# Attention plus experts on one core: the loop over attention chunks written out on four engines

## The chip, the core and the metric

The kernel runs on one core of a Trainium2 chip. The metric is the device time of one execution in microseconds, as the median of several executions. A core has five engines that run their own instruction streams side by side: TensorE (PE in the profile, with PEld for the loads of its stationary operand), VectorE (DVE), ScalarE (ACT), GpSimd (POOL) and SyncE (SP, which here issues DMAs). Each has a sequencer that reads instructions ahead of the engine it feeds; the profile marks rows of a sequencer with a q (PEldq, DVEq). Engines wait for one another through semaphores alone.

## What is computed

One transformer layer over 2048 tokens of width 512. First an attention with a decaying state, then a mixture of 12 experts of which each token takes two. Cut to what matters:

```python
xn = layernorm(x, gamma, beta)
w = sigmoid(xn @ Wx @ Ww + bw); k = xn @ Wk; v = xn @ Wv; r = sigmoid(xn @ Wr)
# 8 heads of 64; one step for each token
def step(state, inp):
    state = (1.0 - wt)[..., None] * state + kt[..., None] * vt[..., None, :]
    y = einsum('bhs,bhst->bht', rt, state)
    return (state, y)
x = layernorm(x + ys @ Wo)
x = layernorm(x + sum over the token's two experts e of cw[e] * (silu(x @ w1[e].T) * (x @ w3[e].T)) @ w2[e].T)
```

## The kernel before

The recurrence is computed in 16 chunks of 128 tokens (`NT` = 16). Two chunks make a pair (`NPAIR` = 8), and the projections of x to decay, key, receptance and value are made for a pair at a time, two or more chunks ahead of their use. On TensorE a call of `chunk` does, for chunk n: the scores of its tokens against each other, by levels of distance (`scores`, L299, 32 products for half of the heads, twice), the reading of the state (L309), the turning of the keys (L329), the output projection of chunk n-1 (L349), the product of scores and values (`apply_values`, L319) and the update of the state (L337). Between these it places the projection jobs of a later pair (`job`, L259 and L270 to L278). Odd chunks take the list `FIRST` (the transposes, then decay and key), even ones the list `SECOND` (receptance and value).

The other engines run their own loop over the same chunks: ScalarE copies out of PSUM and applies sigmoids (`kbT<-pM` at L685 stands once in each chunk), VectorE masks the scores (L831), forms the products of decays (L538, once for a pair) and the levels of receptance (L547, L555), GpSimd forms the levels of the key (L571). ScalarE and GpSimd also split pieces of the expert weights into two halves of 16 bits, three pieces for each chunk; SyncE loads and stores these pieces in a loop of its own (L234).

The order on each engine is the order of the program, and what binds the engines are waits on semaphores with growing counts: the n-th chunk waits for a count that is a multiple of n. Chunk 0 stands ahead of the loop, chunks 13, 14 and 15 behind it. Chunks 1 to 12 are a loop of three rounds with four chunks in its body on TensorE (L427), ScalarE (L779) and VectorE (L936); GpSimd, which works a chunk ahead, has the loop for its chunks 2 to 13 (L964). These are loops of the machine: the body stands once in the program, an engine's register holds the round, each wait on a count and each address that depends on the round is worked out in registers, and at the end of the body a compare-and-branch goes back to its start, twice, and falls through the third time. The experts (from L1137) have loops of the same kind, L1276 on TensorE with 10 rounds, L1492 on VectorE and L1326 on ScalarE with 20, L1568 on GpSimd with 8.

Of the kernel before, what the change touches and what calls it, by code (L numbers as in the profile page):

```python
# [26 lines left out]
NPAIR = T // PAIR  # L27
# [41 lines left out]
def attention(nc, X, idt, kc, gw, x, wxT, ww, wk, wv, wr, wo, by_feature, ident, masks, consts, gate_w, w_experts, w_split, logitT):  # L69
# [9 lines left out]
    with ExitStack() as ctx:  # L79
# [167 lines left out]
        def _(pe):  # L247
# [121 lines left out]
            def chunk(n, k, jobs=None):  # L369

                q, par, slots = jobs or (None, None, [[]] * 5)

                def fill(s):
                    for m in slots[s]:
                        job(q, m, par)
                    if isinstance(n, int) and n in GATE_SLOTS:
                        for u in GATE_SLOTS[n][s]:
                            gate_step(u)
                pe.wait_ge(r_dec, n * NL + (NL - 1))
                pe.wait_ge(r_kept, n * (NL - 2) + (NL - 2))  # L380
                pe.wait_ge(k_dec, n * NL + (NL - 1))
                pe.wait_ge(k_kept, n * (NL - 1) + (NL - 1))
                scores(n, k, 0)
                read_state(n, k)
                turn_keys(n, k)
                if slots is FIRST:
                    job(q, 0, par)
                    job(q, 1, par)
                else:
                    fill(0)  # L390
                if not isinstance(n, int) or n:
                    attend_out(n - 1)
                else:
                    pe.wait_ge(kb_out, 1)
                    pe.sem_inc(m_full, 1)
                if slots is FIRST:
                    fill(0)
                apply_values(n, k, 0)
                scores(n, k, 1)
                fill(1)  # L400
                write_state(n, k)
                fill(2)
                fill(3)
                apply_values(n, k, 1)
                fill(4)
# [18 lines left out]
            pe.wait_ge(setup_done, 1)  # L424
            pe.wait_ge(w_in[5], 16)
            chunk(0, 0, (1, 1, SECOND))
            with pe.Fori(0, (NPAIR - 2) // 2) as j:  # L427
                for u in range(2):
                    chunk(j * 4 + (2 * u + 1), 2 * u + 1, (j * 2 + (2 + u), u, FIRST))
                    chunk(j * 4 + (2 * u + 2), 2 * u + 2, (j * 2 + (2 + u), u, SECOND))  # L430
# [86 lines left out]
        def act_piece(a, n, k, t):  # L517

            _, buf, loaded = piece_of(n, k, t)
            a.wait_ge(piece_in[buf], loaded)  # L520
            if not isinstance(loaded, int) or loaded > 16:
                a.wait_ge(piece_out[buf], loaded - 16)
            a.copy(piece_parts[buf][:, 0, :], piece[buf][:, :]).then_inc(piece_hi, 1)  # L523
# [56 lines left out]
        def pool_chunk(g, n, k, q):  # L580

            for lv in range(NL):
                pool_level(g, n, k, q, lv)
                if lv in PIECE_AT:
                    pool_piece(g, n, k, PIECE_AT.index(lv))
# [3 lines left out]
        def _(a):  # L589
# [186 lines left out]
                        act_piece(a, 0, 0, PIECE_AT.index(at - 5))  # L776
            a.wait_ge(stat1, 9)
            chunk(0, 0, 0, 0, (1, 1, SECOND))
            with a.Fori(0, (NPAIR - 2) // 2) as j:  # L779
                for u in range(2):  # L780
                    q, pair = j * 2 + (2 + u), j * 2 + (1 + u)
                    chunk(j * 4 + (2 * u + 1), 2 * u + 1, j * 2 + u, pair, (q, u, FIRST))
                    chunk(j * 4 + (2 * u + 2), 2 * u + 2, pair, pair, (q, u, SECOND))
# [6 lines left out]
        def _(v):  # L790
# [142 lines left out]
                if lv == 0:  # L933
                    low_x(1, 1)
            chunk(0, 0, nxt=0)
            with v.Fori(0, (NPAIR - 2) // 2) as j:  # L936
                for u in range(2):
                    q, pair = j * 2 + (2 + u), j * 2 + (1 + u)
                    chunk(j * 4 + (2 * u + 1), 2 * u + 1, pair, (q, u))
                    chunk(j * 4 + (2 * u + 2), 2 * u + 2, pair)  # L940
# [12 lines left out]
        @block.gpsimd  # L953
        def _(g):
            for i, name in ((1, "r"), (2, "v")):
                g.wait_ge(w_hi, i + 1)
                g.tensor_tensor(wl[name][:, :, :], staged[name][:, :, :], wh[name][:, :, :], ALU.subtract).then_inc(w_lo[name], 1)

            for name in "krv":
                g.wait_ge(w_lo[name], 1)  # L960
            g.wait_ge(wz_full, KT)
            for n in range(2):
                pool_chunk(g, n, n, 0)
            with g.Fori(0, (NPAIR - 2) // 2) as j:  # L964
                for k in range(2, 6):
                    pool_chunk(g, j * 4 + k, k, j * 2 + k // 2)
            for n in range(NT - 2, NT):
                pool_chunk(g, n, n, n // 2)
# [691 lines left out]
```

## Time and profile before

| what | value |
|---|---|
| runs | 856.07, 857.55 and 864.34 us, median 857.55 |
| the profiled execution | 859.21 us, of which the span of instructions is 857.4 |
| TensorE busy | 725.9 us, 85% of the span |
| VectorE, ScalarE, GpSimd busy | 498.7, 342.1 and 328.7 us |
| granted TensorE clock, mean over the span | 0.932 |
| chunks 1 to 12 (starts of L685, n1 to n13) | 94.45 to 418.54 us |
| expert rounds | about 548 to 796 us |

The profiled execution is 1.7 us above the median of the runs. Times in the rows are microseconds from the start of the span, and durations of single instructions are in nanoseconds where a row says min/median/max. A granted clock of 1.00 is TensorE at its full 2.4 GHz and 0.50 is 1.2 GHz.

### The profile page before, as it was taken

Reading aid. Unit: us, or ns where it says so; the run is one execution under the profiler, and the core shown is the slowest. Engines: PE = TensorE matmul, PEld = TensorE weight load, DVE = VectorE, ACT = ScalarE, POOL = GpSimd, SP = SyncE. Lnnn points to the kernel's source line nnn. Section 1 sums busy time; section 2 is a strip of 40 time slices with the busy share of each in tenths; the row PEclk is TensorE's granted clock in tenths of the full one; section 3 lists DMA queues with packets and bytes.
Section 4 is the critical chain, followed back from the end, with each engine's and each line's share of the span. In section 5 each row is a group of like instructions: output and inputs, shape, how many; then the busy total and the mean of one; then the engine's idle time right before and its main releaser. Section 6 shows DMA issues by size and latency. Waiting matters only on the chain. (4 is left out here: it accounts for less than half of the span.)

```text
span 857.4 us, 18313 instructions
## 1 busy us (share of the span) xinstructions
PE 725.9 (85%) x6030; PEld 525.2 (61%) x6031; DVE 498.7 (58%) x1035; ACT 342.1 (40%) x675; POOL 328.7 (38%) x355
## 2 busy tenths in 40 slices
PE   5879999998999989999969861799999999999400
PEld 2658787876877769778636521466666666666200
DVE  4655867666677646775756558244445444444285
ACT  4454645546345444554466220222222222222154
POOL 0345534542445425454244002243343434333262
PEclk9999999998999989999969975799999999999855
DMA  8615345431454324433342066144466557322394
GB/s 339 225 37 165 117 127 149 148 106 45 149 148 133 105 62 149 141 106 99 101 148 78 22 224 266 50 158 143 165 217 234 197 183 245 122 95 89 134 336 155
DMA packets 38867, 126.75 MB, mean 148 GB/s; under 512 B 3984, under 2 KB 4368, under 8 KB 36496
## 3 DMA queue, kind: packets, MB, share of 16 engines
q1 hardware_dynamic: 31920, 103.31, 35.7%
q0 software_dynamic: 6880, 22.55, 7.7%
q8 instruction: 42, 0.69, 0.3%
q14 instruction: 25, 0.20, 0.1%
HBM read 81.02 MB, written 44.83 MB: 147 GB/s over the span
## 5 line engine op out<-in xcount | busy, mean ns | idle before, releaser
L831 DVE COPY_PREDICATED ST<-msk,pS 128x256 f32<-128x256 uint8 x224 | 121.1, 569 | 100.1 <-issue 65.9
L577 POOL TENSOR_TENSOR piece_parts<-piece,piece_parts 128x1024 f16<-128x1024 f32 x48 | 104.6, 2179 | 115.5 <-ACT piece_parts L523 115.5
L571 POOL TENSOR_TENSOR L<-L,AM 128x256 f32<-128x256 f32 x96 | 70.9, 738 | 118.4 <-ACT L L515 108.8
L1236 PE MATMUL pH<-ring,xgh 128*128 x344 | 104.5, 304 | 5.3 <-issue 2.8
L1237 PE MATMUL pH<-ring,xgh 128*128 x344 | 104.1, 303 | 0.0
L1238 PE MATMUL pH<-ring,xgl 128*128 x344 | 104.1, 303 | 0.0
L299 PE MATMUL pS<-L 64*128 64x64 f32 x1536 | 99.2, 276 | 1.8 <-issue 1.7
L1552 POOL DMA_INDIRECT y_scratch<-ysb,sidx x43 | 42.9, 998 | 136.3 <-DVE ysb L1478 136.3
L299 PEld LDWEIGHTS pS<-L 64*128 64x128 f32 x1536 | 93.6, 192 | 2.1 <-issue 2.1
L1462 DVE TENSOR_TENSOR hid<-pH,sil 128x320 f32<-128x320 f32 x43 | 21.1, 492 | 119.6 <-ACT sil L1315 119.6
L555 DVE TENSOR_TENSOR L<-L,AM 128x256 f32<-128x256 f32 x96 | 70.6, 735 | 16.1 <-ACT L L502 10.0
L1315 ACT ACTIVATE sil<-pH 128x320 f32<-128x320 f32 x43 | 18.8, 437 | 131.0 <-PE pH L1238 131.0
L349 PE MATMUL pM<-w_o,yT 128*128 128x512 f32 x128 | 59.8, 611 | 4.3 <-ACT yT L724 2.8
L523 ACT CAST piece_parts<-piece 128x1024 f16<-128x1024 f32 x48 | 50.1, 1043 | 24.4 <-DMA piece<-in_w_experts 24.4
L1539 POOL DMA_INDIRECT xg<-x_scratch,gidx x43 | 42.7, 994 | 34.0 <-POOL gidx L1536 30.8
L1254 PE MATMUL pO<-ring,hTh 128*128 x129 | 49.0, 380 | 1.8 <-DVE hTh L1473 1.4
L1255 PE MATMUL pO<-ring,hTh 128*128 x129 | 48.9, 379 | 0.0
L1236 PEld LDWEIGHTS pH<-ring,xgh 128*128 128x128 f16 x344 | 34.0, 99 | 24.3 <-issue 11.1
L502 ACT COPY L<-L 128x256 f32<-128x256 f32 x80 | 32.5, 407 | 38.2 <-DVE L L555 26.9
L1311 ACT CAST hTh<-pHT 128x384 f16<-128x384 f32 x43 | 20.6, 479 | 63.9 <-PE pHT L1244 63.9
L1478 DVE COPY ysb<-pO 128x512 f32<-128x512 f32 x43 | 29.7, 692 | 23.0 <-PE pO L1255 23.0
L1237 PEld LDWEIGHTS pH<-ring,xgh 128*128 128x128 f16 x344 | 33.9, 99 | 13.4
(206 smaller groups left out, 1623.6 us busy)
## 6 DMA issues: line engine op xcount, KB each, us to landing
piece<-in_w_experts SPq DMA_DIRECT2D x48, 512.0 KB, 5.5
w_split_scratch<-piece_parts SPq DMA_DIRECT2D x48, 512.0 KB, 3.9
ring<-w_split_scratch SPq DMA_DIRECT2D x12, 2048.0 KB, 8.6
yin<-y_scratch SPq DMA_DIRECT2D x16, 512.0 KB, 5.8
x_scratch<-X SPq DMA_DIRECT2D x1, 4096.0 KB, 14.1
out_x<-X SPq DMA_DIRECT2D x8, 512.0 KB, 2.8
X<-in_x SPq DMA_DIRECT2D x1, 3072.0 KB, 23.3
X<-in_x SPq DMA_DIRECT2D x2, 512.0 KB, 7.5
```

The lines of the kernel that those rows point to most:

```text
L299: i = pe.matmul(o, k_, r_, start=True, stop=True)
L349: i = pe.matmul(pM[:, 0, :], yT[:, g, :], w_o[:, g, :], start=(g == 0), stop=(g == KT - 1))
L523: a.copy(piece_parts[buf][:, 0, :], piece[buf][:, :]).then_inc(piece_hi, 1)
L555: v.tensor_tensor(next_grown(k, lv, 1), grown(rec, k, lv, 1), factor(c, lv, 0), ALU.mult).then_inc(r_dec, 1)
L571: g.tensor_tensor(next_kept(k, lv, 0), kept(key, k, lv, 0), by, ALU.mult).then_inc(k_dec, 1)
L577: g.tensor_tensor(piece_parts[buf][:, 1, :], piece[buf][:, :], piece_parts[buf][:, 0, :], ALU.subtract).then_inc(piece_lo, 1)
L831: v.copy_predicated(out[:, :, :, 0 if lv == 0 else 1, :], msk[:, lv, :, :].rearrange(shape, m=m), pS[:, :, lv * S:(lv + 1) * S].rearrange( ...
L1236: pe.matmul(p[:, 0, 0:F], xgh[par][:, k, :], wh, start=(k == 0), stop=False)
L1237: pe.matmul(p[:, 0, 0:F], xgh[par][:, k, :], wl, start=False, stop=False)
L1238: t = pe.matmul(p[:, 0, 0:F], xgl[par][:, k, :], wh, start=False, stop=(k == KT - 1))
L1254: pe.matmul(pO[:, 0, :], hTh[:, k, :], wh, start=(k == 0), stop=False)
L1255: t = pe.matmul(pO[:, 0, :], hTh[:, k, :], wl, start=False, stop=(k == FT - 1))
```

## The change

In the four engines' programs the loop of the machine is replaced by a loop of Python, so that each of the twelve chunks stands in the program with its own numbers. SyncE's program and the expert loops stay as they are.

```diff
@@ TensorE
-            with pe.Fori(0, (NPAIR - 2) // 2) as j:
+            for j in range((NPAIR - 2) // 2):
                 for u in range(2):
                     chunk(j * 4 + (2 * u + 1), 2 * u + 1, (j * 2 + (2 + u), u, FIRST))
                     chunk(j * 4 + (2 * u + 2), 2 * u + 2, (j * 2 + (2 + u), u, SECOND))
@@ ScalarE
-            with a.Fori(0, (NPAIR - 2) // 2) as j:
+            for j in range((NPAIR - 2) // 2):
@@ VectorE
-            with v.Fori(0, (NPAIR - 2) // 2) as j:
+            for j in range((NPAIR - 2) // 2):
@@ GpSimd
-            with g.Fori(0, (NPAIR - 2) // 2) as j:
+            for j in range((NPAIR - 2) // 2):
                 for k in range(2, 6):
                     pool_chunk(g, j * 4 + k, k, j * 2 + k // 2)
```

The start of a round on TensorE before the change. These rows stand once in the program and are reached from chunk 0 and, twice, from the branch at the end of the body:

```order
L427 UNCONDITIONAL_BRANCH
L427 ISA
L380 ISA [waits r_dec]
L382 ISA [waits k_dec,r_kept]
L285 ISA [waits k_kept]
L299 MATMUL pS<-rec,key 128x64 [waits s_dve]
L299 MATMUL pS<-rec,key 128x64
L299 MATMUL pS<-rec,L 128x64 x2
L299 MATMUL pS<-L 128x64 x12
```

And the end of the body, behind the last projection job of the round:

```order
L316 REGISTER_ALU
L319 MATMUL pY<-ST,val 64x128 [waits s_dve]
L319 MATMUL pY<-ST,val 64x128 x3
L427 REGISTER_ALU
L427 COMPARE_AND_BRANCH
```

The same place after the change, between chunks 4 and 5. `ISA` rows at the head of a chunk are sequencer instructions that wait or set registers; the branch and they are gone, and the waits sit on the first matmul of the scores:

```order
L278 MATMUL pA<-wh_v,xl 128x512
L319 MATMUL pY<-ST,val 64x128 [waits s_dve]
L319 MATMUL pY<-ST,val 64x128 x3
L299 MATMUL pS<-rec,key 128x64 [waits k_kept,k_dec,s_dve,r_kept,r_dec]
L299 MATMUL pS<-rec,key 128x64
L299 MATMUL pS<-rec,L 128x64 x2
```

No matmul has moved against another. On VectorE the end of the body stood like this:

```order
L872 TENSOR_TENSOR state<-pM,sdec 64x4x64
L880 ISA [waits x1_ready]
L880 BN_STATS stats<-X 128x6
L936 REGISTER_ALU
L936 COMPARE_AND_BRANCH
```

and the branch led to the products of decays, with a register instruction ahead of nearly each of them:

```order
L936 ISA
L531 ISA [waits a_out]
L538 TENSOR_TENSOR AM<-dec 128x512 [waits r_dec,k_dec]
L535 ISA
L538 TENSOR_TENSOR AM<-AM 128x256 [waits am_ready]
L535 REGISTER_ALU
L538 TENSOR_TENSOR AM<-AM 128x128 [waits am_ready]
```

After the change these two pieces join, and what is left between them are the operations themselves:

```order
L872 TENSOR_TENSOR state<-pM,sdec 64x4x64
L880 BN_STATS stats<-X 128x6 [waits x1_ready]
L538 TENSOR_TENSOR AM<-dec 128x512 [waits r_dec,k_dec,a_out]
L538 TENSOR_TENSOR AM<-AM 128x256 [waits am_ready]
L538 TENSOR_TENSOR AM<-AM 128x128 [waits am_ready]
```

Here too the order of the operations is the same as before; only the branch, the register arithmetic and the separate waits have gone. SyncE's rows are the same in both programs.

## Rows read from the trace of the kernel before

**Rows 1.** The page: span, granted TensorE clock in 40 slices, TensorE's instruction queue.

```profile
span 857.4 us, 18313 instructions
...
PEclk9999999998999989999969975799999999999855
...
q8 instruction: 42, 0.69, 0.3%
```

**Rows 2.** Timeline of ScalarE, 60 to 300: start, us, what, idle before, releaser.

```profile
204.05 0.59 ACT L685 COPY kbT<-pM 128x512 f32<-128x512 f32 x1 [5.39 <-PE pM L329]
```

**Rows 3.** Windows between starts of L685: length, busy by engine, PEclk, DMA share, GB/s.

```profile
121.47:146.46 24.99, 24.99 (x246) 18.78 (x245) 18.44 (x35) 12.77 (x26) 11.65 (x10) 1.00 0.44 127
146.46:173.48 27.02, 26.21 (x278) 21.91 (x277) 17.82 (x29) 14.32 (x31) 12.25 (x10) 1.00 0.37 118
173.48:204.05 30.57, 27.46 (x246) 21.00 (x245) 18.87 (x37) 12.94 (x26) 11.21 (x10) 0.90 0.36 106
...
231.13:256.12 24.99, 24.99 (x246) 18.77 (x245) 18.71 (x35) 12.77 (x26) 11.67 (x10) 1.00 0.45 128
256.12:283.15 27.03, 26.22 (x278) 21.93 (x277) 17.85 (x29) 14.33 (x32) 12.28 (x10) 1.00 0.37 118
283.15:314.51 31.36, 28.36 (x246) 21.88 (x245) 18.59 (x37) 12.93 (x26) 11.27 (x10) 0.89 0.36 104
...
393.55:418.54 24.99, 24.95 (x244) 18.51 (x242) 19.18 (x35) 11.44 (x25) 11.70 (x10) 1.00 0.43 128
418.54:452.04 33.50, 24.65 (x202) 16.82 (x203) 18.70 (x43) 19.72 (x37) 11.54 (x10) 0.80 0.30 95
```

**Rows 4.** Line L427 on TensorE's sequencer: duration min/median/max in ns, first to last start.

```profile
L427 PEldq COMPARE_BRANCH  x3: 76/3638/5121, 190.4 to 410.5; - x3
```

**Rows 5.** Line L936 on VectorE's sequencer, 297 to 307.

```profile
L936 DVEq COMPARE_BRANCH  x1: 63/63/63, 299.0 to 299.0; - x1
L936 DVEq FUSED_REGOPS  x1: 85/85/85, 304.9 to 304.9; - x1
```

**Rows 6.** Line L779 on ScalarE's sequencer, 297 to 307.

```profile
L779 ACTq FUSED_REGOPS  x1: 78/78/78, 303.2 to 303.2; - x1
```

**Rows 7.** Timeline of TensorE, 188 to 204.

```profile
194.62 0.44 PE L299 MATMUL pS<-rec,key 64*128 64x64 f32 x4 [1.42 <-issue]
...
199.18 1.98 PE L299 MATMUL pS<-L 64*128 64x64 f32 x17 [1.68 <-issue]
201.09 2.07 PE L309 MATMUL pY<-L,state 128*128 128x128 f32 x8
```

**Rows 8.** Timeline of TensorE, 142 to 149.

```profile
144.83 1.16 PE L309 MATMUL pY<-L,state 128*128 128x128 f32 x8
```

**Rows 9.** Timeline of VectorE, 138 to 204.

```profile
138.33 1.40 DVE L538 TENSOR_TENSOR AM<-dec 128x512 f32<-128x512 f32 x1
...
194.38 0.69 DVE L538 TENSOR_TENSOR AM<-dec 128x512 f32<-128x512 f32 x1 [3.96 <-issue]
```

**Rows 10.** Windows behind the two taken back branches (columns of Rows 3).

```profile
198.10:204.90 6.80, 5.72 (x35) 5.60 (x35) 2.99 (x6) 1.41 (x4) 0.66 (x1) 0.50 0.01 2
307.30:314.10 6.80, 6.71 (x53) 6.43 (x50) 3.26 (x9) 0.74 (x2) 0.66 (x1) 0.50 0.03 11
```

**Rows 11.** DMA queues that load instructions, 560 to 790: packets, MB, share.

```profile
q8 instruction: 1, 0.02, 0.0%
q14 instruction: 2, 0.02, 0.0%
```

**Rows 12.** Lines of the expert loops' branches on TensorE's and VectorE's sequencers.

```profile
L1276 PEldq COMPARE_BRANCH  x10: 76/207/238, 571.6 to 788.0; - x10
...
L1492 DVEq COMPARE_BRANCH  x20: 50/56/74, 567.5 to 795.6; - x20
```

**Rows 13.** Waits of TensorE, 80 to 470: total us, times, longest.

```profile
PE pA L270 <- DVE xl L816: 4.5, 6, 0.8
```

**Rows 14.** Line L316 on TensorE's sequencer.

```profile
L316 PEldq ALU_OP  x24: 32/32/32, 100.3 to 408.6; - x24
```

## The prediction

> **What bounds the kernel now.** I began with the page [rows 1]: the span is 857.4 us, and and the granted clock is at full speed from the first slice to the 20th, with two exceptions, a digit 8 in the tenth and one in the fifteenth. Each slice is 21.4 us, so these lie near 200 and 310 us, in the midst of the attention chunks. Such a dip is a place to look. Next I cut the stage at an event that occurs once in each chunk, ScalarE's copy at L685, of which there are 16 from 71.79 to 474.51 (one is shown in [rows 2]), and asked for the busy time between them [rows 3]. The reader should compare lengths of like chunks. A stretch from the copy of an even chunk to that of the next odd one lasts 24.99 us, and TensorE is busy for all 24.99 of it; a stretch that starts in an odd chunk lasts 27.02 with 26.21 busy. So inside a round TensorE is the bound, at full clock. Two stretches are out of line, and they are the two that hold a taken back branch: 30.57 us (chunk 4 to 5) and 31.36 us (chunk 8 to 9). The third even stretch at the end of a round, 12 to 13, has the branch that falls through, and lasts 24.99 like the rest.
>
> **Why those two are long.** TensorE's branch instruction itself [rows 4]: of its three executions one took 76 ns, the others 3638 and 5121 ns. On VectorE the branch record is short, but the next sequencer instruction came at 304.9 behind a branch at 299.0, 5.9 us later [rows 5]; ScalarE, whose branch came at 303.0, went on at 303.2 [rows 6]. Then the timelines. TensorE stood idle for 1.42 us ahead of the first scores of the new round and for 1.68 us in the midst of them [rows 7], neither put down to another engine. Behind that gap its matmuls ran slowly: the same eight state reads took 2.07 us [rows 7] against 1.16 in an ordinary chunk [rows 8]. The granted clock in the 6.8 us behind each gap was 0.50, the 1.2 GHz level [rows 10], after TensorE had stood idle at the branch. VectorE sat idle 3.96 us ahead of its first product of decays, where in the round before it went on without a gap [rows 9].
>
> **What is removed.** The price of a taken back branch needs no model, since the same chunk without one is in the same trace. First: 30.57 - 24.99 = 5.58 us. Second: 31.36 - 24.99 = 6.37 us. The busy column says what they are made of. Idle time: 30.57 - 27.46 = 3.11 and 31.36 - 28.36 = 3.00. Work made longer by the lower clock: 27.46 - 24.99 = 2.47 and 28.36 - 24.99 = 3.37. The sums agree with the 5.58 and 6.37 [rows 3]. All of it is on the path, because TensorE is the engine that is never idle in the ordinary stretch, so **11.95 us** go. VectorE's stall goes with it and takes nothing more: it waits for TensorE's scores there in any case. The loop's entry and its fall-through cost 0: the stretch 12 to 13 is no longer than its like [rows 3].
>
> The queue of TensorE's instructions moved 42 packets in all [rows 1], and only one in the 230 us of the expert rounds [rows 11], whose ten branches took at most 238 ns [rows 12]: a short loop is not loaded again, and the long one is. The Trainium skill, page "Runtime: NRT & Kernel Launch", section "Instruction fetch mechanics", says that a taken branch to code which the sequencer no longer holds must wait until that code is fetched by DMA; by that rule the change takes away just these waits, and the trace agrees with it.
>
> **What is added.** Nothing that executes. But the code of chunks 5 to 12 is now new code, loaded once each, instead of the body passed again. The bound comes from the first round, which even before the change was code passed for the first time: its stretches of 24.99 and 27.02 us equal those of the second round, 24.99 and 27.03 [rows 3]. So a straight passage through fresh instructions hides its loads; I take 0, and at the far end 0.01 us for each of the eight chunks, 0.1 us.
>
> **What else goes: register arithmetic and separate waits.** TensorE's 24 additions at L316 took 32 ns each [rows 14], 0.8 us if every one were on the path, and the other engines shed some such instructions ahead of most operations. In the even stretches TensorE has no idle time at all, so nothing can be gained there. In the odd ones it waits for the low part of x, 0.8 us at most, 4.5 us over six chunks [rows 13], on a chain through ScalarE and VectorE. I take 0, because this chain's operations run back to back; the far ends are a gain of 4.5 us and the loss of 0.1 that stands above. The fourth and longest stretch, 33.50 us with a mean clock of 0.80 [rows 3], is chunk 13, which stood outside the loop already. It keeps its code, but starts 12 us earlier, and where its low-clock time falls may change. By the two stretches above, one such lapse made work 2.47 to 3.37 us longer; I take 0 and keep 3.4 us to either side.
>
> **The sum.** 857.4 - 11.95 = 845.4 us of span, and 859.2 - 11.95 = 847.3 us for the profiled execution. That one stood 1.7 us above the median; for the median I forecast 857.55 - 11.95 = **845.6 us**, a gain of 1.4%. What comes after the attention is a chain in which nothing waits for a fixed time, so it should begin 12 us sooner and last as long.
>
> **Rivals.**
> *The full gain and more.* ScalarE and VectorE, with their register instructions gone, close TensorE's wait in the odd chunks too: 845.6 - 4.5 = 841.1. Against it: the wait is one of operations and not of issue. Chance 0.07.
> *A lapse of the clock in its place.* A gap in chunk 13, or behind it, costs one more stretch at the lower clock: 845.6 + 3.4 = 849.0. For it: the digits 6, 7, 5 and 7 between the 21st and the 26th slice [rows 1] say that this region has several. Chance 0.10.
> *The gap is no matter of the branch.* The expert pieces' transfers run at the same time, and TensorE's gap might stay with them. Then 857. Against it, the stretches without a branch have such transfers as well (GB/s of 118 to 128 against 104 and 106) and no gap [rows 3]. Chance 0.04. To the same time leads a rule of price: if a taken branch cost what a fall-through does, 76 ns, the change would give 0.2 us, 857.4. The Trainium skill, page "Advanced Engine Details and Errata", section "Control Flow Timing", gives about 108 ns for a compare-and-branch; the 3638 and 5121 ns here are far off that, and the 207 ns of the expert loop are near it. So I give the rule nothing for these two branches.
> *Slower: the expert loops are reloaded.* The written-out program is longer, so the expert loops stand at other places in the instruction stream. They are short enough now to stay loaded [rows 11, 12]; if one of them came to lie so that its start is lost at each round, each of TensorE's nine taken branches at L1276 would cost 5.58 to 6.37 us, 50 to 57 us: 896 to 903. Break-even is at two such branches. Against it: each body keeps its length, and over ten and twenty passes the queues brought one packet for TensorE and two for all others together, so there seems to be room to spare. Chance 0.03. Straight code that starves where the loop did not, with more than 12 us lost, gets 0.02: the first round speaks against it.
> The forecast, 845.6 within some 2 us, has the remaining 0.74.
>
> **How the numbers follow.** No change cannot be told from a change of less than 1% in this kernel, 8.6 us. The forecast and the first rival lie beyond that. The lapse rival, at 849.0, is 8.55 us faster and splits evenly: 0.05 to either side. Faster than 848.97 therefore has 0.74 + 0.07 + 0.05 = 0.86, of which I take off 0.02 for the scatter of the runs (856.07 and 857.55 are 1.5 us apart), 0.84. Within 1% has 0.05 + 0.04 + 0.02 = 0.11, and slower 0.05. The range must reach the forecast and the two nearby rivals: down to 841.1, up to 849.0, and 0.5 us of scatter at the upper end, 841 to 849.5.
>
> **What would show it.** In the changed kernel's profile the even stretches between L685 copies, 4 to 5 and 8 to 9, should be 25.0 us with TensorE busy throughout and a clock of 1.00; the idle times of 1.42, 1.68 (TensorE) and 3.96 us (VectorE) should be gone; TensorE's instruction queue should still show some 40 packets. Copies n5 and n9 should start at 198.5 and 302.6 us, n13 at 406.6. The forecast is wrong if a stretch of straight code is longer than its like, if the odd stretches shrink, if chunk 13 takes other than 33.5 us, or if the expert rounds on VectorE no longer last the (795.6 - 567.5) / 19 = 12.0 us of [rows 12].

## The result

The changed kernel runs in 846.68 us (median of 4 runs, 845.40 to 846.88), the kernel before in 856.97 us (median of 4, 856.07 to 864.34). The ratio of the runs is 0.9846 with a 95% interval of 0.9805 to 0.9887, faster by 1.5%; the two medians alone are 10.29 us or 1.2% apart. Forecast were 1.4% and 845.6 us. Compared again with more runs (`e11_after_again`), the two stood at 847.65 and 858.61 us, 10.96 us apart, ratio 0.9868, interval 0.9837 to 0.9899. One execution of the kernel before, timed beside `e12_pe_both`, took 1274.15 us at a mean granted clock of 0.577 and enters no number below. The profiled execution took 846.87 us with a span of 844.6; 847.3 and 845.4 were forecast for it.

The page of the changed kernel, the lines that answer to [rows 1]:

```profile
span 844.6 us, 17397 instructions
...
PEclk9999999999999999999979975899999999999755
...
q8 instruction: 37, 0.61, 0.3%
```

The 8 in the tenth slice and the one in the fifteenth are gone. TensorE's instruction queue (q8) moved 37 packets where it had moved 42: the code is longer, and less of it is loaded. `e4_two_rounds` below shows that this count goes with the taken branches.

ScalarE's copies L685 cut the stage as before. The windows between them, with the columns of [rows 3]:

```profile
174.04:199.03 24.99, 24.99 (x246) 18.79 (x245) 18.38 (x35) 12.76 (x27) 11.65 (x10) 1.00 0.41 128
199.03:226.05 27.02, 26.22 (x278) 21.91 (x277) 17.86 (x29) 14.31 (x32) 12.16 (x10) 1.00 0.35 118
...
278.06:303.05 24.99, 24.99 (x246) 18.77 (x245) 18.14 (x35) 12.75 (x27) 11.66 (x10) 1.00 0.41 128
...
407.07:441.53 34.46, 25.07 (x202) 16.25 (x203) 18.55 (x43) 19.71 (x37) 11.53 (x10) 0.80 0.28 92
```

The two stretches of 30.57 and 31.36 us now last 24.99 each, TensorE busy in all of it. Odd stretches kept their 27.02. From copy n1 to copy n13 the stage took 418.54 - 94.45 = 324.09 us before and 407.07 - 95.00 = 312.07 now, 12.02 less.

TensorE's timeline where the first back branch was, to be read beside [rows 7] and [rows 8]; the idle time would stand in brackets at the end of a row, and there is none:

```profile
193.09 0.66 PE L319 MATMUL pY<-ST,val 128*64 128x128 f32 x8
193.68 0.44 PE L299 MATMUL pS<-rec,key 64*128 64x64 f32 x4
...
197.40 1.16 PE L309 MATMUL pY<-L,state 128*128 128x128 f32 x8
```

And VectorE's, which had stood idle for 3.96 us here [rows 9]:

```profile
190.26 0.69 DVE L880 BATCH_NORM_STATS2 stats<-X 128x6 f32<-128x512 f32 x1
190.87 1.30 DVE L538 TENSOR_TENSOR AM<-dec 128x512 f32<-128x512 f32 x1
```

The expert loops were not disturbed by their new place, as the branch row of TensorE shows beside [rows 12]:

```profile
L1276 PEldq COMPARE_BRANCH  x10: 76/208/226, 559.4 to 774.8; - x10
```

### The profile page after: what moved, and what is told of

Read it like the earlier page. It is cut to its first block and busy times, and to the rows that moved or that the text cites. A ratio compares the mean times of both kernels' runs of the same rounds, so it can differ in the third digit from the quotient of the medians.

```text
span 844.6 us, 17397 instructions
## 1 busy us (share of the span) xinstructions
PE 718.4 (85%) x6030; PEld 519.4 (61%) x6031; DVE 497.3 (59%) x1035; ACT 341.4 (40%) x675; POOL 328.1 (39%) x355
## 5 line engine op out<-in xcount | busy, mean ns | idle before, releaser
L299 PE MATMUL pS<-L 64*128 64x64 f32 x1536 | 96.2, 271 | 0.0
L299 PEld LDWEIGHTS pS<-L 64*128 64x128 f32 x1536 | 91.1, 188 | 0.0
L1236 PEld LDWEIGHTS pH<-ring,xgh 128*128 128x128 f16 x344 | 33.8, 98 | 24.8 <-issue 11.5
L270 PE MATMUL pA<-xh,wh_z 128*128 128x256 f16 x128 | 34.9, 273 | 8.6 <-DVE xl L816 4.8
```

Of the source, the lines that this page charges most:

```text
L299: i = pe.matmul(o, k_, r_, start=True, stop=True)
L1236: pe.matmul(p[:, 0, 0:F], xgh[par][:, k, :], wh, start=(k == 0), stop=False)
```

## The experiments

All were timed beside the kernel before. Since a few microseconds are at stake, each is also read by the time from copy n1 to copy n13, in which the loop lies; it is 324.09 us before the change and 312.07 after it, and the later stages don't enter it. It is known for one execution of each kernel, the profiled one. `e7_light_loads` and `e10_light_straight` leave most of the expert weights out of the computation.

| kernel | median us | ratio (interval) | n1 to n13 | stretch 4 to 5 | stretch 8 to 9 |
|---|---|---|---|---|---|
| before | 857.0 to 859.1 | 1 | 324.09 | 30.57 | 31.36 |
| change | 846.68 | 0.9846 (0.9805 to 0.9887) | 312.07 | 24.99 | 24.99 |
| e11_after_again | 847.65 | 0.9868 (0.9837 to 0.9899) | 312.08 | 24.99 | 24.99 |
| e1_pe_only | 847.03 | 0.985 (0.9804 to 0.9896) | 313.01 | 25.28 | 24.99 |
| e2_dve_only | 858.40 | 0.9996 (0.997 to 1.0021) | 325.39 | 32.92 | 30.39 |
| e3_pe_dve | 846.85 | 0.9851 (0.9808 to 0.9894) | 312.07 | 24.99 | 24.99 |
| e4_two_rounds | 855.35 | 0.9942 (0.9913 to 0.9971) | 317.78 | 30.68 | 24.99 |
| e5_gap_long | 859.93 | 0.9997 (0.9964 to 1.003) | 328.46 | 33.14 | 33.21 |
| e6_gap_short | 849.89 | 0.988 (0.9834 to 0.9927) | 318.75 | 26.24 | 30.36 |
| e7_light_loads | 848.34 | 0.989 (0.9832 to 0.9948) | 315.56 | 26.65 | 26.82 |
| e10_light_straight | 842.87 | 0.981 (0.977 to 0.985) | 312.07 | 24.99 | 25.00 |
| e8_experts_out | 842.98 | 0.9805 (0.9768 to 0.9842) | 312.09 | 24.99 | 24.99 |
| e9_pe_experts | 843.66 | 0.9817 (0.9783 to 0.985) | 312.09 | 25.00 | 24.99 |
| e12_pe_both | 843.16 | 0.9819 (0.978 to 0.9859) | 312.62 | 25.00 | 24.99 |

### Which engine's branch

`e1_pe_only`: TensorE's loop alone is written out.

```diff
--- before
@@ TensorE
-            with pe.Fori(0, (NPAIR - 2) // 2) as j:
+            for j in range((NPAIR - 2) // 2):
```

> Only TensorE's loop is written out; VectorE, ScalarE and GpSimd keep theirs. Theory A (TensorE's own reload is the price): TensorE's idle times of 3.1 and 3.0 us and the low clock behind them go, the stretches between copies n4 to n5 and n8 to n9 fall from 30.57 and 31.36 to 25 us, and the time falls by 11 to 12 us, as with all four written out. Rival B (VectorE's reload is the price and TensorE's only lies beside it): VectorE still stalls 4 to 5 us ahead of its decay products, its masks come late, TensorE waits for them, and the gain is under 6 us. In ordinary stretches VectorE waits 2.4 us for the scores behind those products; a stall of 3.96 and 5.14 us is longer than that, so something between, a gain of 8 to 11 us with stretches of 25.5 to 27.5 us, would say that VectorE's stall was hidden by TensorE's and comes to light without it.

It had nearly the whole gain: 847.03 us. The first back branch's stretch and the one after it, and the same at the second:

```profile
173.68:198.96 25.28, 25.28 (x249) 19.08 (x248) 17.05 (x35) 12.89 (x26) 10.67 (x9) 1.00 0.40 127
198.96:226.37 27.41, 26.04 (x276) 21.62 (x274) 18.16 (x31) 14.50 (x32) 13.68 (x11) 1.00 0.36 116
...
303.37:330.66 27.29, 26.22 (x278) 21.92 (x277) 18.02 (x30) 14.51 (x32) 13.55 (x11) 1.00 0.37 117
```

The first branch's two stretches are 0.29 and 0.39 us above 24.99 and 27.02, and behind the second branch only one is longer, by 0.27 us: 0.95 us in all. VectorE in the same kernel shows where that comes from:

```profile
194.76 0.69 DVE L538 TENSOR_TENSOR AM<-dec 128x512 f32<-128x512 f32 x1 [4.15 <-issue]
...
198.29 1.32 DVE L831 COPY_PREDICATED ST<-msk,pS 128x256 f32<-128x256 uint8 x2
```

It still stalls at its own branch, for 4.15 us, and its masks begin without a wait of their own. So VectorE's pause was covered by TensorE's, and uncovered it is worth 0.68 and 0.27 us, where my band of stretches allowed 0.5 to 2.5 a branch.

`e2_dve_only`: the same edit on VectorE's loop alone.

> Only VectorE's loop is written out. Theory A: TensorE still reloads its code at both branches, nothing is gained, 0 to 1 us, and the two stretches stay at 30 to 31.4 us. Rival B: the stretches shrink by 3 us or more.

Nothing was gained, 858.40 beside 858.69 us. Of the two stretches one was longer than in the profile of before and one shorter:

```profile
174.29:207.21 32.92, 29.68 (x246) 23.36 (x245) 20.07 (x37) 12.85 (x26) 11.64 (x10) 0.84 0.33 99
...
286.24:316.63 30.39, 27.62 (x246) 21.11 (x245) 19.57 (x37) 12.85 (x27) 11.65 (x10) 0.89 0.38 106
```

The range of 30 to 31.4 that I wrote was too narrow for one of them. Four stretches with a taken branch, from two kernels, now read 30.4 to 32.9: the price of one such branch is 5.4 to 7.9 us and changes from pass to pass. The idle part is steadier, 32.92 - 29.68 = 3.24 and 30.39 - 27.62 = 2.77 us, beside 3.11 and 3.00 before; most of the difference is work at the lower clock. In the longer stretch the granted clock stood at 0.50 for 10.2 us (196.8 to 207.0), in the shorter one for 6.8 us (309.4 to 316.2).

`e3_pe_dve`: both edits, ScalarE's and GpSimd's loops kept.

> TensorE's and VectorE's loops are written out, ScalarE and GpSimd keep theirs. Theory A (with or without a hidden stall of VectorE): the full gain, 11 to 12.5 us, because the other two went through their branches within 0.3 us. A rival, that the gain came from register arithmetic on ScalarE and GpSimd, would leave a part of it out.

846.85 us and 312.07 us between the copies, the same as the change to the hundredth. The loops of ScalarE and GpSimd cost nothing.

`e4_two_rounds`: all four engines loop over two rounds, and the third is written out.

```diff
--- before
@@ TensorE, and in the same way ScalarE, VectorE and GpSimd
-            with pe.Fori(0, (NPAIR - 2) // 2) as j:
+            with pe.Fori(0, 2) as j:
                 ...
+            for j in range(2, 3):
+                for u in range(2):
+                    chunk(j * 4 + (2 * u + 1), 2 * u + 1, (j * 2 + (2 + u), u, FIRST))
+                    chunk(j * 4 + (2 * u + 2), 2 * u + 2, (j * 2 + (2 + u), u, SECOND))
```

> On all four engines the loop keeps two rounds, and the third is written out behind it: one taken back branch in place of two. If each taken branch has its price, about half of the gain: 5.6 to 6.4 us less than the kernel before, the stretch n4 to n5 at 30 to 31.5 us and n8 to n9 at 25.0. If the gain came from having constants in place of registers, the third round alone would have it, 4 us, and n8 to n9 would stay long.

One taken branch is left, and one long stretch:

```profile
L427 PEldq COMPARE_BRANCH  x2: 79/1768/3458, 190.3 to 300.0; - x2
```

```profile
173.35:204.03 30.68, 27.47 (x246) 21.00 (x245) 18.99 (x37) 12.95 (x27) 11.17 (x10) 0.90 0.38 106
...
283.08:308.07 24.99, 24.99 (x246) 18.78 (x245) 18.57 (x35) 12.76 (x26) 11.65 (x10) 1.00 0.44 128
```

TensorE's queue of instructions, on this kernel's page, stands between the 42 packets with two taken branches and the 37 with none:

```profile
q8 instruction: 39, 0.64, 0.3%
```

It is 42 as well in `e2_dve_only`, which keeps both of TensorE's branches, and 37 in `e1_pe_only` and `e3_pe_dve`, which have none. So a taken branch of TensorE back over the long body does load code again. The second queue of instructions, q14, moved 25 packets before the change and in `e1_pe_only`, and 17 in `e2_dve_only`, where VectorE's loop is gone: VectorE's branch does the same.

Between the copies it gained 324.09 - 317.78 = 6.31 us, as expected. The median gained only 858.69 - 855.35 = 3.3, less than I wrote; in the profiled execution chunks 13 and 14 took 58.85 us (412.10 to 470.95) where they took 55.97 before (418.54 to 474.51), which hides 2.9 us of the gain. That constants in place of registers made the gain is excluded: chunks 1 to 4 run on registers and chunks 9 to 12 on constants here, in the same 24.99 and 27.02 us.

### Is it the code or the pause

`e5_gap_long` and `e6_gap_short` take the written-out kernel and put a pause of TensorE alone where the branches were.

```diff
--- after
@@ TensorE, chunk
+                if n in (5, 9):
+                    pe.wait_ge(k_dec, (n + 1) * NL + 2)      # e5_gap_long
+                    pe.wait_ge(r_dec, (n + 1) * NL + 1)      # e6_gap_short
                 scores(n, k, 0)
```

(one of the two added waits in each kernel)

> The written-out kernel with a pause put in where the back branches were: ahead of the scores of chunks 5 and 9 TensorE also waits for GpSimd's second product for the next chunk, which in an ordinary round ends some 2.8 us later. No code is loaded again. If idle time alone drops the clock, as I read the kernel before, each pause costs its 2.8 us and 2.5 to 3.4 us of slower work: 10.6 to 12.4 us in all, back to 857 to 859. If the lower clock belonged to the reload, the two pauses cost 5.6 us and no more, about 852.

> The same with a shorter pause: ahead of the scores of chunks 5 and 9 TensorE waits for VectorE's first product of the next chunk, which ends about 1 us later. Expected: 2 us in all, with a clock of 1.00 in the stretches behind, 848 to 849; if even a pause of 1 us drops the clock, 7 to 9 us, 854 to 856.

The long pause came out longer than planned, 3.51 us. TensorE's timeline at the first, and the windows of both stretches:

```profile
193.92 0.66 PE L319 MATMUL pY<-ST,val 128*64 128x128 f32 x8
198.09 0.69 PE L299 MATMUL pS<-rec,key 64*128 64x64 f32 x4 [3.51 <-POOL L L573]
```

```profile
174.87:208.01 33.14, 29.63 (x246) 23.32 (x245) 19.36 (x37) 12.75 (x27) 11.66 (x10) 0.85 0.32 96
...
287.05:320.26 33.21, 29.70 (x246) 23.40 (x245) 19.63 (x37) 12.74 (x27) 11.66 (x10) 0.85 0.31 96
```

The first scores behind the pause took 0.69 us against 0.44 in the changed kernel, the granted clock was 0.50 from 197.6 to 207.7 us, and busy time rose by 29.63 - 24.99 = 4.64 us without one instruction more: the queue of instructions moved 37 packets as in the changed kernel, and the clock fell all the same. So idle time of TensorE at this place is enough to bring the lower clock, and 3.5 us of it cost 8.2 both times. The two together cost the kernel its whole gain, 859.93 us.

The short pause, at both places:

```profile
195.05 0.44 PE L299 MATMUL pS<-rec,key 64*128 64x64 f32 x4 [1.17 <-DVE L L549]
```

```profile
300.57 0.44 PE L299 MATMUL pS<-rec,key 64*128 64x64 f32 x4 [1.43 <-DVE L L549]
```

```profile
174.16:200.40 26.24, 25.07 (x246) 18.80 (x245) 18.03 (x35) 12.75 (x27) 11.65 (x10) 1.00 0.39 121
...
279.43:309.79 30.36, 28.93 (x246) 22.64 (x245) 19.41 (x37) 12.75 (x26) 11.65 (x10) 0.86 0.34 105
```

One pause, of 1.17 us, cost 1.25 and left the clock at 1.00; the other, of 1.43, cost 5.37, with a granted clock of 0.50 from 301.4 to 311.6 us. I had expected both to behave alike. The profiled execution was the longest of its four (853.39 us at a mean clock of 0.934, beside 849.38 to 850.10 at 0.939 to 0.941), so the other three paid less for the lower clock.

### What the traffic does to a reload

`e7_light_loads` keeps the loops and takes most of the expert pieces' loads away; `e10_light_straight` is the same kernel with the four loops written out.

```diff
--- before
@@ SyncE
-                sp.dma_start(piece[i % 2][:, :], w_experts[bass.ds(e, 1), :, i * PIECE:(i + 1) * PIECE]
+                sp.dma_start(piece[i % 2][:, :FEW], w_experts[bass.ds(e, 1), :, i * PIECE:i * PIECE + FEW]
...
+            sp.wait_ge(setup_done, 1)
@@ VectorE, at the start
+            for buf in piece:
+                v.memset(buf[:, :], 0.0)
```

> The kernel before, its loops kept, but each piece of expert weights is loaded with 64 of its 1024 columns, the rest being zeros; the stores stay whole. If the second branch took 5.1 us instead of 3.6 because its code came through queues full of the pieces' data, both branches now take 2 to 3.5 us and each of the two long stretches falls to 29 to 30 us. If a reload has a price of its own, independent of other traffic, they stay at 3.3 to 5.5 us and 30 to 33 us. Of the computation most of the expert weights are left out.

> The written-out kernel with the light loads (64 of 1024 columns of each piece, the rest zeros; most of the expert weights are left out of the computation). Beside the loop kernel with the same loads it shows the price of two taken branches without that traffic. From the stretches there (26.65 and 26.82 us against 24.99): 3.5 us less than it between copies n1 and n13, all stretches at 24.99 and 27.02. The rival that the traffic itself slows ordinary stretches would make stretches here shorter than 24.99.

(The added lines move L427 to L429, L299 to L301 and L309 to L311.) The records of the two taken branches are 3.80 and 3.98 us, between the 3.64 and 5.12 of the kernel before, but the rest of the price shrank:

```profile
L429 PEldq COMPARE_BRANCH  x3: 76/3802/3975, 190.0 to 401.5; - x3
```

```profile
194.35 0.44 PE L301 MATMUL pS<-rec,key 64*128 64x64 f32 x4 [1.59 <-issue]
...
198.07 1.16 PE L311 MATMUL pY<-L,state 128*128 128x128 f32 x8
```

```profile
173.05:199.70 26.65, 25.06 (x246) 18.79 (x245) 17.98 (x35) 12.85 (x27) 11.24 (x10) 1.00 0.20 66
...
278.74:305.56 26.82, 25.06 (x246) 18.78 (x245) 17.96 (x35) 12.84 (x27) 11.45 (x10) 1.00 0.19 66
```

The pause ahead of the first scores is there, 1.59 us, as in [rows 7] with 1.42. What is missing is the second pause in the midst of the scores, the 1.68 us of [rows 7]. TensorE idles for 26.65 - 25.06 = 1.59 and 26.82 - 25.06 = 1.76 us in all, where under full loads it was 2.8 to 3.2, and the clock stays at 1.00: the state reads take 1.16 us. Each taken branch costs 1.66 and 1.83 us here in place of 5.58 and 6.37. Both of my guesses were off: the branches did not get shorter, and the stretches fell far below 29 us.

The traces hold the instruction queue's packets one by one, and they show what goes with the second pause. In the kernel before, the first packet behind the branch record (190.40) started at 191.34 and took 1.21 us, the second started at 196.89 and took 0.94, and TensorE's second pause ended at 199.18. With light loads the branch record starts at 189.97, the first packet at 190.92 (1.37 us) and the second already at 194.51 (0.96 us). So the packets were not carried more slowly under full loads; the second one started 5.55 us behind the first in place of 3.59. In between, from 192.5 to 196.9, the 16 engines were busy for 85% of the time, mostly with the pieces' queue (q1). The window 195 to 196 of the kernel before, then its window 196 to 197, then 194 to 195 with light loads:

```profile
q1 hardware_dynamic: 38, 0.16, 82.9%
...
q8 instruction: 1, 0.02, 5.9%
...
q8 instruction: 1, 0.02, 6.0%
```

The other two passes with a pause in the midst of the scores have the same late second packet, 5.32 us behind the first in e4 and 5.61 in e2; at the second light branch it was 3.74. In the two passes with one long pause, 2.90 and 3.25 us, two packets started together, within 0.3 us, and took 1.4 to 2.7 us.

The light kernel's price of 1.66 and 1.83 us is that of its fastest execution, though. The four took 844.14, 845.28, 851.40 and 855.03 us, at mean granted clocks of 0.940, 0.941, 0.932 and 0.928. Two of them, then, ran with more of the lower clock under the same light loads. Where it lay in them isn't known. What the traces show of the light loads is the shorter idle time; that they also spare the lower clock holds for the profiled execution alone.

With the loops written out the same light kernel took 312.07 us between the copies, 3.49 less, which is the 3.5 expected, and ordinary stretches are 24.99 and 27.02 with or without the traffic. In the medians it is 848.34 to 842.87, 5.5 us, and the other kernel's runs lie between 842.17 and 844.02.

### The short branches of the expert loops

`e8_experts_out`: the written-out kernel with the four expert loops written out too. `e9_pe_experts`: only TensorE's of them. `e12_pe_both`: from the kernel before, TensorE's two loops and no others.

```diff
--- after
@@ TensorE, experts (e9_pe_experts; in e8_experts_out the loops of the other three as well)
-            with pe.Fori(0, rounds) as j:
+            for j in range(rounds):
```

> The written-out kernel with the expert loops of TensorE, ScalarE, VectorE and GpSimd written out too. Their branches take 50 to 208 ns and reload nothing. If the rule is that only a reload costs, this gives nothing that can be measured: 0 to 2 us less than with the attention loop alone, 844.5 to 847. If register arithmetic held these loops up, it would give 5 us or more. A loss would be code that now has to be loaded where it lay ready: over 849.

> The written-out kernel with TensorE's expert loop alone written out too; VectorE, ScalarE and GpSimd keep theirs. In the kernel with all expert loops written out, TensorE's ten waits of 0.3 to 0.5 us at the start of a tile behind its branch were gone, and waits for gathered rows came in their place. If TensorE's own branch and register work made the gain of 3.7 us, this has it too, 842.5 to 844.5. If the other three engines' loops made it, this stays at 846 to 847.5.

> The changed kernel as it is, once more, on the chip of the two others and with more rounds: 845.5 to 848, a ratio of 0.984 to 0.988. All its runs should lie within 3 us of each other, where those of the kernel before spread over 8: if what varies from run to run is the reload at the two branches, it is gone here.

> Only TensorE's two loops are written out, the attention's and the experts'; VectorE, ScalarE and GpSimd keep all of theirs. If the two gains belong to TensorE and add, this stands at 843 to 845.5, level with the kernels in which four engines were written out, save about 1 us for VectorE's reload in the attention. If not, it stays at 846 or more.

The waits of TensorE between 550 and 780 us, with the total, the count and the longest, in the changed kernel:

```profile
PE pH L1236 <- issue: 3.2, 10, 0.5
```

in the one with all expert loops written out:

```profile
PE pX L1217 <- DMA xg<-x_scratch,gidx: 4.2, 5, 1.2
```

and in the one with TensorE's alone:

```profile
PE pX L1217 <- DMA xg<-x_scratch,gidx: 2.8, 5, 1.0
```

I had expected 0 to 2 us from the first of these and it gave 3.7, 842.98 against the change's 846.68. TensorE's loop alone gave 847.65 - 843.66 = 4.0 us on the same chip, with no overlap of the runs (840.24 to 845.02 beside 846.80 to 848.79), so the other three contribute nothing that shows. The ten waits of up to 0.5 us at a round's first tile are gone, but waits at L1217 stand in their place: 4.2 us for gathered rows in e8, and 2.8 us for them with 1.1 us of issue in e9. The rounds themselves became less than 4 us shorter. From the first to the last start of L1217 they took 253.0 us in the changed kernel and 253.1 when it was run again, and 251.7, 252.1 and 252.0 in e9, e8 and `e12_pe_both`, 0.9 to 1.4 us less. So the gain in the medians is shown, and that TensorE's loop makes it; that it is what TensorE waited for behind the ten branches is not, and where the rest of it lies is open. The loads of the longer code cost nothing that shows: q8 moved 52 packets in these three kernels, 15 more than in the changed one. `e12_pe_both`, with two edited lines, reached 843.16 us and a ratio of 0.9819: the two gains belong to TensorE and add. VectorE's uncovered pause cost it 312.62 - 312.07 = 0.55 us, and it is level with the fastest kernels here that compute all of the layer.

`e11_after_again` lay in its expected band, with all six runs between 846.80 and 848.79, 2.0 us apart. The eleven runs of the kernel before beside it lay between 856.23 and 864.09, 7.9 us apart. The light kernels show the same, 10.9 us with the loops and 1.9 without. But it is not the reload as such that varies: the kernel with two long pauses and no reload has it too, 856.12 to 864.39, 8.3 us. The scatter comes with the pauses, and each execution's mean granted clock says by which part. In the kernel with two long pauses the shortest execution had 0.936 and the longest 0.925; in the kernel before, beside `e11_after_again`, 856.23 us went with 0.933 and 864.09 with 0.925. By and large the longer executions are those with more of the lower clock.

## Why the prediction was right

**The price from like chunks.** 11.95 us were to go, by the difference of two stretches to their ordinary length. Between the copies 12.02 went, and both stretches came to exactly the ordinary length. Nothing else in the working carried as much. That the price sits in the branch is shown by e4 (one branch, 6.31 us) and e1, and that code is loaded again there by the packets of q8, 42, 39 and 37.

**What the sum's good fit owes to luck.** For the profiled execution 847.3 us were forecast and 846.87 came. The span became 12.8 us shorter where 11.95 were forecast: 12.02 in the loop and 1.94 behind chunk 14, less 0.55 by which copy n1 started later (95.00 beside 94.45) and 0.61 that chunks 13 and 14 took more. The working had these last three at 0, and most of them cancels. The medians fell by less than the loop did, 10.29 and 10.96 us, and they move by more than a microsecond from one comparison to the next. The loop's entry was put at 0 from stretch 12 to 13, which can't show it; the stretch that can, n0 to n1, took 22.66 us before and 22.65 after.

**Idle time and lower clock.** The split into 3.1 and 3.0 us of idle time and 2.5 and 3.4 of slower work held in kind: e5 gives the second part with no reload at all. The first 0.50 of [rows 10] did not begin behind the gap, as I wrote, but within it: at 198.10, while the second pause lasted until 199.18. What I did not see is that only 1.6 to 1.8 us of idle time are there with light loads; the other 1.2 to 1.5 us came with the pieces' full loads (e7). The rival that traffic alone makes the gap was rightly put low, since written-out code runs through the same traffic with none. But with the full loads a taken branch cost 5.4 to 7.9 us in five passes, and with light ones 1.66 and 1.83 us in the one execution profiled.

**VectorE takes nothing more.** True for the change, since both pauses go at once; e1 sizes what TensorE's had covered at 0.95 us for two branches, so "takes nothing more" holds only while TensorE's branch goes too.

**Straight code hides its loads.** Held: chunks 5 to 12, now loaded fresh, run in 24.99 and 27.02 us. The bound of 0.1 us was not needed.

**Register arithmetic worth 0.** Held: the odd stretches kept 27.02 us and their 0.8 us of idle time, and ScalarE's and GpSimd's loops cost nothing (e3).

**Chunk 13.** It took 34.46 us in place of 33.50. I had named "other than 33.5 us" as a sign that the forecast is wrong, and by that sign it failed here, though 0.96 us lie well within the 3.4 us kept for this chunk. The mean clock was 0.80 as before, and chunk 14 took 22.12 in place of 22.47. In the kernels with full loads the two together took 53.9 to 59.3 us (e1 and e2). The term of 3.4 us to either side was the right size for it. The other signs held: the odd stretches kept their length, and VectorE's expert rounds lasted 11.9 us ((782.4 - 555.5) / 19) where 12.0 were forecast. The median forecast, 845.6, lies 1.1 us below the measured 846.68.

**The slower rival.** The expert loops were not reloaded. But their short branches were waved through too lightly: I noted 207 ns as near the nominal price, and did not ask what TensorE's loop costs beside it. Writing it out took 4.0 us off the median (e9), of which the rounds show 0.9 to 1.4. This did not enter the forecast, as the change leaves these loops alone. The Trainium skill, page "Advanced Engine Details and Errata", section "Control Flow Timing", gives about 108 ns for a compare-and-branch. An estimate from that figure for ten of them is 1.1 us. The records here are longer, 208 ns in the median, and the whole loop was worth 4.0 us in e9.

## What to carry to other kernels

Where a machine loop's body is long and the engine that bounds the kernel runs it, compare the stretch across the back edge (the taken branch from the end of the body to its start) with one inside the body: the difference is what writing the loop out gave here, 11.95 us read beforehand and 12.02 found in the traces, 10.3 to 11.8 in the medians (the smallest for the change, the largest for e3). Do it first for the bounding engine alone; one changed line on TensorE gave all but 0.94 us (e1; 0.55 in `e12_pe_both`) of what the four engines' did between the copies, and a second one the gain of the expert loop. A pause of TensorE must be priced with the slower work behind it, 8.2 us for 3.5 here, so a small stall in a busy stage is worth more than its own length.

## What was not expected of the hardware

The same taken branch cost 1.66 and 1.83 us in the profiled execution with light loads and 5.4 to 7.9 us with the full ones, through nearly twice the idle time and, in these traces, the lower clock behind it. The added idle time stood in a second pause (1.68 us in the kernel before, 1.68 in e2, 1.97 in e4) or in one longer pause (2.90 and 3.25). That the pieces' loads bring it is shown. With the second pause went a second instruction packet that started 5.3 to 5.6 us behind the first in place of 3.6 to 3.7, while data packets filled the DMA engines. That it stood in line behind them is argued only, since the trace has no time at which it was asked for.

Of four single pauses at that place, those of 1.17, 1.59 and 1.76 us left the clock at 1.00 and the one of 1.43 us was followed by a granted clock of 0.50; so were both of 3.51 us. Length alone does not decide among the short ones, and what else does is open.

The first branch record of 3.80 us on TensorE's sequencer (e7) went with only 1.59 us of idle time of the engine. The record starts at 190.0, and the engine was busy with matmuls that stand ahead of the branch until 192.8: the record is not the price.
